# A graph attention layer's gather: visits of 64 target nodes instead of 125

## The chip, the cores and the metric

One core of one Trainium2 chip runs the whole program in one launch. The metric is device time in microseconds (us), here the median of three runs. A profiled execution of the same program gives the trace.

## The reference

The program is a graph attention layer with a residual, then a top-2 mixture of eight experts with a residual. The change concerns the first.

```python
xp = (x @ W).reshape(N, H, C)                 # N=3125 nodes, H=4 heads, C=256, 1024 columns in
a_src, a_dst = einsum(xp, att_src), einsum(xp, att_dst)          # N x H each
src, dst = edge_index[0] + loops, edge_index[1] + loops          # E=50000 edges, sorted by dst
e = leaky_relu(a_src[src] + a_dst[dst], 0.2)
m = segment_max(e, dst)
ee = exp(e - m[dst]); z = segment_sum(ee, dst)
out = segment_sum(xp[src] * (ee / z[dst])[:, :, None], dst)
x = x + relu(out + bias)                      # x was layer-normed before; then the experts
```

## The kernel before

The 3125 nodes are 25 **blocks** of 125, the 50,000 edges 391 **tiles** of 128. The edges are sorted by target, so a block's edges are consecutive; a tile that holds the border of two blocks is **visited** once for each, 391 + 25 = 416 visits in all. A visit takes 128 edges in the 128 partitions and adds what they bring to the sums of one block. Four visits are a group (104 groups).

**Projection** (0 to about 342 us, L303 to L714). For each tile of 125 nodes: layer norm on DVE (L458 to L487), transposes and products on PE (L664 to L683), high and low half-precision parts of the result (ACT L395, DVE L493), the terms of the nodes (DVE L508). POOL stores two arrays of 125 rows of 4096 bytes for each of the 25 tiles (L378, L380), and the stage of the layer's end one more. Between these, tile by tile and by hand (L624 to L654), DVE prepares the visits: 24 counts of edges below a block's border (`count`, L513, three in each of tiles 2 to 9), the visits' blocks and the words that tell where one begins and ends (`visits`, tile 11), the edges' numbers within their block (`edge_numbers`, tile 13; POOL fetches them with eight small gathers after tile 9, L370), three turns, eight parts of one-hots of the high part of the source (`high_one_hots`, L598, tiles 17 to 24), and the first chunk's tables (`build_first`, L609).

**Tables** (335 to 483 us, L760 to L875). In 8 chunks of 13 groups the node terms are selected for each edge: DVE turns numbers into one-hots in place (`build`, L776, L777: 128 x 6656 each), PE multiplies them with the terms (L865, L870), DVE picks and totals (L790, L800). SP loads the two arrays of each chunk (L767).

**Maxima and weights** (483 to 552 us, L895 to L1018). The result is PK: for each visit and edge the local target number (125 targets), the weights' high parts, a one, the weights' low parts.

**Gather** (552 to 1303 us, L1023 to L1145), the stage in question:
- POOL copies four columns of source numbers (L1047), waits for the row buffer's last use (`s_done`), and issues one indirect DMA a visit (L1052), 128 rows of 4096 bytes: the source's projected row, high part and low part. There are eight row buffers.
- DVE copies the group's packed weights (L1075, L1076), makes a one-hot of the target (L1083), and multiplies it with the four heads' high weights (L1087); ACT does the same with the low weights (L1113). Four buffers hold the one-hots, so DVE waits for `s_done` of the visit four before (L1082).
- PE adds into PSUM, for each head: high one-hot x high row, high x low, low x high, each 128 x 128 by 256 columns (L1130), then one product of 96 columns for the sums of the weights (L1135).
- At the end of a block DVE copies the sums to SBUF (`take`, L1066 twice 512 columns, L1067). It looks for ends after every second visit. PE waits before the first product of a new block until its half of PSUM is free:

```python
if first and h % 2 == 0 and not early(v, 1):
    pe.wait_ge(s_seen, 3 * v - 2 + h // 2)
for a, b in ((0, 0), (0, 1), (1, 0)):
    pe.matmul(main_ps[:, h * C:(h + 1) * C], O[:, k, 1 + HEADS * a + h, :],
              rows[:, 4 * p + k, b, h * C:(h + 1) * C], ...)
```

**Layer's end** (1303 to 1602 us), then **experts** (56 tiles of 128 slots, 7168 slots for 6250 pairs). The experts' three indirect DMAs a tile (L1403, L1726, L1732) carry `bounds_check=NODES - 1, oob_is_err=False`; empty slots have a number out of bounds. In that stage DVE splits the experts' weights with `scalar_tensor_tensor` on two SBUF operands (L1426) and also works with one operand in PSUM (L1757, L1767).

## Time and profile before

| what | value |
|---|---|
| median of 3 runs | 2163.4 us (2161.5 to 2164.1) |
| span of the profiled execution, first to last instruction | 2296.1 us |
| the profiled execution's own time | not given beside the span |
| busy in the span: PE, DVE, ACT, POOL | 1959.2, 1470.6, 1137.3, 768.2 us |
| mean granted clock of PE | 0.919 |
| DMA | 490.15 MB, mean 213 GB/s |

The rows are read so: a line number with L is a line of the kernel before; PE is TensorE, DVE VectorE, ACT ScalarE, POOL GpSimd, SP SyncE. A group's busy time is the union of its instructions, its mean that of one; the idle time is that of the engine just before them, with what ended it. "issue" is a wait for nothing that the profile shows. The granted clock is a share of 2.4 GHz.

### The profile page before, as it was taken

The page shows a single profiled execution, that of the slowest core. Times are in us where ns is not written, and L with a number is a line of the kernel's source. Part 1 is how long each engine was busy: PE and PEld are TensorE (multiplying, and loading weights), DVE is VectorE, ACT ScalarE, POOL GpSimd, SP SyncE. Part 2 cuts the span into 40 slices and gives each one's busy share as a digit, 9 for nine tenths or more (in the row PEclk, how much of TensorE's full clock was granted, in tenths as well). Part 3 has the DMA queues.
Part 4 walks back from the last instruction along what each step waited for, and adds up shares of the span by engine and source line. Part 5 has one row for each costly group of instructions (what it writes and reads, how often), then busy time and mean ns, then how long its engine had stood idle before and what let it go on. Part 6 is the DMA issues. An engine that isn't in the chain of part 4 may idle for free. (4 is left out here: it accounts for less than half of the span.)

```text
span 2296.1 us, 53233 instructions
## 1 busy us (share of the span) xinstructions
PE 1959.2 (85%) x14846; PEld 1318.7 (57%) x14847; DVE 1470.6 (64%) x4341; ACT 1137.3 (50%) x2499; POOL 768.2 (33%) x943
## 2 busy tenths in 40 slices
PE   6999977667878888888888589983899999999997
PEld 4666545645766667777667455652454445555553
DVE  7988859987666666666666699867543443443333
ACT  4444421113666666676666566654543443443332
POOL 1020000022555555555555232321233333333332
PEclk9999976568999999999999889995899999999999
DMA  7444544403988888888888677746646556644542
GB/s 272 134 143 136 172 131 172 186 0 114 312 281 291 286 299 287 294 296 287 287 298 294 235 249 240 228 142 234 233 169 249 212 167 239 221 160 171 176 162 80
DMA packets 135664, 490.15 MB, mean 213 GB/s; under 512 B 16900, under 2 KB 17108, under 8 KB 133410
## 3 DMA queue, kind: packets, MB, share of 16 engines
q0 software_dynamic: 95568, 334.62, 43.5%
q1 hardware_dynamic: 31954, 125.15, 15.1%
q10 hardware_dynamic: 8064, 29.36, 3.7%
q8 instruction: 47, 0.77, 0.1%
q14 instruction: 31, 0.25, 0.0%
HBM read 419.17 MB, written 81.17 MB: 218 GB/s over the span
## 5 line engine op out<-in xcount | busy, mean ns | idle before, releaser
L1130 PE MATMUL main_ps<-rows,O 128*128 128x256 f16 x4992 | 619.2, 283 | 125.7 <-DVE acc L1066 66.3
L1113 ACT ACTIVATE O<-O,pk 128x128 f16<-128x128 f16 x1664 | 502.9, 387 | 246.1 <-DVE O L1083 203.5
L1130 PEld LDWEIGHTS main_ps<-rows,O 128*128 128x128 f16 x4992 | 480.9, 102 | 217.9 <-issue 72.8
L1052 POOL DMA_INDIRECT rows<-projected,idx x416 | 395.5, 951 | 325.2 <-PE small_ps L1135 202.9
L1087 DVE TENSOR_SCALAR O<-O,pk 128x128 f16<-128x128 f16 x1664 | 314.6, 273 | 15.0 <-issue 0.2
L1837 PE MATMUL x_h<-w_p,gram 128*128 x1344 | 307.1, 386 | 18.4 <-ACT gram L1787 7.6
L1852 PE MATMUL x_o<-w_p,gram 128*128 x1344 | 308.0, 379 | 1.4 <-ACT gram L1806 1.4
L1886 PE MATMUL pj_ps<-gram,xsT 128*125 128x512 f16 x1200 | 271.1, 385 | 8.8 <-ACT xsT L402 5.5
L1837 PEld LDWEIGHTS x_h<-w_p,gram 128*128 128x128 f16 x1344 | 131.6, 99 | 171.6 <-issue 31.5
L1886 PEld LDWEIGHTS pj_ps<-gram,xsT 128*125 128x125 f16 x1200 | 163.2, 139 | 104.7 <-ACT xsT L402 8.6
L1083 DVE TENSOR_SCALAR O<-iota,pk 128x128 f16<-128x128 f16 x416 | 109.4, 263 | 164.9 <-PE small_ps L1135 124.1
L1852 PEld LDWEIGHTS x_o<-w_p,gram 128*128 128x128 f16 x1344 | 129.2, 98 | 147.1 <-issue 1.6
L1795 ACT ACTIVATE h_g<-h_b 128x512 f32<-128x512 f32 x56 | 35.3, 630 | 301.7 <-DVE h_b L1767 301.7
L1732 POOL DMA_INDIRECT out_dram<-x_y,xi x56 | 57.5, 1027 | 349.8 <-DVE x_y L1760 349.8
L1895 PE MATMUL n_pj<-gram,PK 128*128 128x512 f16 (+3 forms) x900 | 156.2, 330 | 13.3 <-ACT PK L1343 13.3
L1757 DVE SCALAR_TENSOR_TENSOR x_o<-x_o,b_t 128x1024 f32<-128x1024 f32 x56 | 69.0, 1233 | 135.4 <-PE x_o L1852 132.2
L1787 ACT ACTIVATE gram<-x_tr 128x2048 f16<-128x2048 f16 x56 | 105.1, 1878 | 58.3 <-PE x_tr L1904 55.0
L1895 PEld LDWEIGHTS n_pj<-gram,PK 128*128 128x128 f16 x900 | 83.8, 99 | 82.5 <-ACT PK L1343 15.9
L1760 DVE SCALAR_TENSOR_TENSOR x_y<-x_o,gate_of_slot,x_y 128x1024 f32<-128x1024 f32 x56 | 71.9, 1284 | 69.4 <-DMA x_y<-out_dram,xi 62.1
L1217 POOL TENSOR_TENSOR PK<-n_xn,PK 125x1024 f16<-125x1024 f32 x25 | 53.3, 2130 | 165.6 <-DVE n_x L1267 151.7
L1767 DVE SCALAR_TENSOR_TENSOR h_b<-x_h,b_b 128x512 f32<-128x512 f32 x56 | 38.7, 690 | 107.1 <-PE x_h L1837 104.3
L378 POOL DMA_DIRECT2D projected_f<-xp_f x25 | 13.2, 527 | 247.7 <-ACT xp_f L396 247.7
(346 smaller groups left out, 2538.9 us busy)
## 6 DMA issues: line engine op xcount, KB each, us to landing
w_f<-in_L_ffn_W_dram SPq DMA_DIRECT2D x14, 2048.0 KB
b_t<-in_L_ffn_b_dram ACTq DMA_DIRECT2D x56, 512.0 KB
projected_f<-xp_f POOLq DMA_DIRECT2D x25, 500.0 KB, 3.7
projected<-xp POOLq DMA_DIRECT2D x25, 500.0 KB, 4.6
out_dram<-n_x SPq DMA_DIRECT2D x25, 500.0 KB
x_after_gnn_normed<-PK POOLq DMA_DIRECT2D x25, 500.0 KB, 9.1
xt<-in_x_dram SPq DMA_DIRECT2D x24, 512.0 KB, 3.3
n_own<-projected_f SPq DMA_DIRECT2D x24, 512.0 KB, 13.0
```

Of the source, the lines that this page charges most:

```text
L1052: pool.indirect_dma_start(out=rows[:, 4 * p + k, :, :].rearrange("k n d -> k (n d)"), out_offset=None, in_=xp_d[:, :], in_offset=bass.Indi ...
L1083: dve.tensor_scalar(O[:, k, 0, :], iota16[:, :], pk[:, p, k, 0:1], None, ALU.is_equal).then_inc(s_oh, 1)
L1087: ins = dve.tensor_scalar(O[:, k, 1 + h, :], O[:, k, 0, :], pk[:, p, k, 1 + h:2 + h], None, ALU.mult)
L1113: ins = act.activation(O[:, k, 1 + HEADS + h, :], O[:, k, 0, :], ACT.Copy, scale=pk[:, p, k, w:w + 1])
L1130: pe.matmul(main_ps[:, h * C:(h + 1) * C], O[:, k, 1 + HEADS * a + h, :], rows[:, 4 * p + k, b, h * C:(h + 1) * C], start=first and h % 2 ...
L1757: dve.scalar_tensor_tensor(o_ps[:, p, :], o_ps[:, p, :], 1.0 / WS, b2_t[:, p, :], ALU.mult, ALU.add).then_inc(s_ob, 1)
L1760: dve.scalar_tensor_tensor(y[:, p, :], o_ps[:, p, :], at1(gateT, i), y[:, p, :], ALU.mult, ALU.add).then_inc(s_eo, 1)
L1787: act.activation(xgT[:, p, :, :, :], tr_ps[:, :, :, :], ACT.Copy).then_inc(s_xT, 1)
L1837: ins = pe.matmul(h_ps[:, :], xgT[:, p, a, k, :], w, start=(k == 0 and a == b), stop=(k == KD - 1 and a == 1))
L1852: ins = pe.matmul(o_ps[:, p, n * 512:(n + 1) * 512], hT[:, p, a, f, :], w, start=(f == 0 and a == b), stop=(f == KF - 1 and a == 1))
L1886: ins = pe.matmul(out, lhs[:, a, k, :], rhs[:, b, k, :], start=(k == 0 and a == b), stop=(k == last - 1 and a == 1))
L1895: ins = pe.matmul(out[:, cols], lhs[:, a, k, :], rhs[:, b, k, cols], start=(k == 0 and a == b), stop=True, skip_group_check=True)
```

## The change

A visit now serves one **sub-block**: nodes 0 to 63 or 64 to 124 of a block, 50 in all; 391 + 49 = 440 visits, 110 groups, 10 chunks of 11 groups. The stationary operand of a product holds a head's high and low one-hots side by side, 64 + 64 columns; two products a head (with the high and the low row) put the sums of both in the two halves of PSUM's partitions, one PSUM array for even and one for odd sub-blocks. One `scalar_tensor_tensor` on DVE makes all nine one-hots of a visit, in one of eight buffers; ACT has no part in the stage. At a block's end DVE moves one half across the partitions and adds the other, for both sub-blocks. Edges of a tile that lie outside the visit's sub-block get a source number past the last node, except in the first eight visits (visit = 4 x partition + q there, and `far` is zero in partitions 0 and 1), and the DMA's bounds check leaves them out. The counts are 49, five a tile in tiles 2 to 11, and what follows them moves by two tiles; the high one-hots come in five parts in tiles 20 to 24; the terms are copied once more, by sub-block.

```diff
-VISITS = TILES + BLOCKS
+SUB = 64
+SUBS = 2 * BLOCKS
+VISITS = TILES + SUBS - 1
...
-CHUNK = VISITS // 8
+CHUNKS = 10
+CHUNK = VISITS // CHUNKS
...
+SEEN = 9
...
-            PER = 3
+            PER = 5
...
-                        if i == 9:
+                        if i == 11:
                             rows_by_visit()
...
+                        dve.tensor_scalar(far[:, :], iota_col[:, :], 1.5, float(NODES), ALU.is_gt, ALU.mult)
+                        dve.tensor_scalar(out_f, fV[:, 3, :], -0.5, None, ALU.is_lt)
+                        link(dve.tensor_scalar(past_f, fV[:, 3, :], SUB - 0.5, None, ALU.is_gt))
+                        link(dve.tensor_tensor(out_f, out_f, past_f, ALU.add))
+                        dve.scalar_tensor_tensor(fV[:, 0, :], out_f, far[0:VP, :], fV[:, 0, :], ALU.mult, ALU.add).then_inc(s_vals, 1)
...
+                    def by_sub(n, bs):
+                        dve.wait_ge(s_st16, 2 * n + 2)
+                        dve.wait_ge(s_sub0, 1)
+                        of = st_sub[:, :, :].rearrange("k (b n) a -> k n b a", n=2)
+                        dve.tensor_copy(of[0:SUB, 0, bs, :], st16[0:SUB, bs, :])
+                        dve.tensor_copy(of[0:ROWS - SUB, 1, bs, :], st16[SUB:ROWS, bs, :])
...
-                        if 2 <= i < 10:
-                            for b in range(PER * (i - 2) + 1, PER * (i - 1) + 1):
+                        if 2 <= i < 12:
+                            for b in range(PER * (i - 2) + 1, min(PER * (i - 1) + 1, SUBS)):
                                 count(b)
...
-                        if i == 11:
+                        if i == 13:
                             visits()
-                        if i == 13:
+                        if i == 15:
                             edge_numbers()
-                        if i in (15, 17, 19):
-                            turned_numbers((i - 15) // 2)
+                        if i in (17, 18, 19):
+                            turned_numbers(i - 17)
...
-                        if 17 <= i < 25:
-                            high_one_hots(i - 17)
+                        if 20 <= i < 25:
+                            high_one_hots(i - 20)
...
-            O = sbuf(c, "O", [P, 4, 1 + 2 * HEADS, P], F16)
+            O = sbuf(c, "O", [P, 8, 1 + 2 * HEADS, SUB], F16)
...
-                                in_offset=bass.IndirectOffsetOnAxis(ap=idx[:, p, k:k + 1], axis=0)).then_inc(s_row[4 * p + k], 16)
+                                in_offset=bass.IndirectOffsetOnAxis(ap=idx[:, p, k:k + 1], axis=0),
+                                bounds_check=NODES - 1, oob_is_err=False).then_inc(s_row[4 * p + k], 16)
...
+                        for odd, own, off in ((0, low, up), (1, up, low)):
+                            for half in (slice(0, 512), slice(512, D)):
+                                dve.tensor_copy(other[own, half], main_ps[off, odd, half]).then_inc(s_seen, 1)
+                                n = n + 1
+                                wait_apart(dve, s_met, s_seen, n)
+                                dve.tensor_tensor(a(half)[own], main_ps[own, odd, half], other[own, half], ALU.add).then_inc(s_seen, 1)
+                                n = n + 1
+                            if odd == 0:
+                                for to, half_of in ((low, 0), (up, 1)):
+                                    ins = dve.tensor_copy(at(sacc, b)[to], small_ps[up, half_of, 0:2 * SUMS])
+                                ins.then_inc(s_seen, 1)
+                                n = n + 1
+                        wait_apart(dve, s_met, s_seen, n)
...
-                            if not early(i, 1):
-                                dve.wait_ge(s_done, v - 3)
-                            dve.tensor_scalar(O[:, k, 0, :], iota16[:, :], pk[:, p, k, 0:1], None,
-                                              ALU.is_equal).then_inc(s_oh, 1)
-                            dve.wait_ge(s_oh, v + 1)
-                            for h in range(HEADS):
-                                ins = dve.tensor_scalar(O[:, k, 1 + h, :], O[:, k, 0, :], pk[:, p, k, 1 + h:2 + h],
-                                                        None, ALU.mult)
-                            ins.then_inc(s_hi, 1)
+
+                            dve.scalar_tensor_tensor(
+                                O[:, 4 * p + k, :, :], iota16[:, 0:SUB].unsqueeze(1).broadcast_to([P, 1 + 2 * HEADS, SUB]), pk[:, p, k, 0:1],
+                                pk16[:, p, k, 1:2 + 2 * HEADS].unsqueeze(2).broadcast_to([P, 1 + 2 * HEADS, SUB]),
+                                ALU.is_equal, ALU.mult).then_inc(s_oh, 1)
...
-                @block.scalar
-                def _(act):
-                    def body(i, j, p):
-                        for k in range(4):
-                            act.wait_ge(s_oh, 4 * i + k + 1)
-                            for h in range(HEADS):
-                                w = 1 + SUMS + h
-                                ins = act.activation(O[:, k, 1 + HEADS + h, :], O[:, k, 0, :], ACT.Copy, scale=pk[:, p, k, w:w + 1])
-                            ins.then_inc(s_lo, 1)
...
-                                pe.wait_ge(s_seen, 3 * v - 2 + h // 2)
-                            for a, b in ((0, 0), (0, 1), (1, 0)):
...
+                                pe.wait_ge(s_seen, SEEN * (v - 1) + 2 + h)
+                            cols = slice(h * C, (h + 1) * C)
+                            for b in range(2):
+                                pe.matmul(of(main_ps, cols), O[:, 4 * p + k, 2 * h:2 * h + 2, :].rearrange("k n c -> k (n c)"),
+                                          rows[:, 4 * p + k, b, cols],
+                                          start=first and h % 2 == 0 and b == 0, stop=True, skip_group_check=True)
```

## Rows read from the trace of the kernel before

**Rows 1.** Stretches: us, busy of PE, PEld, DVE, ACT, POOL, clock, DMA share, GB/s.

```profile
74.10:85.00 10.90, 10.90 (x64) 7.07 (x63) 10.25 (x36) 5.15 (x9) 1.05 (x2) 1.00 0.50 145
129.90:140.40 10.50, 10.50 (x63) 7.05 (x62) 8.22 (x28) 5.14 (x8) 1.04 (x2) 1.00 0.50 147
...
335.40:482.70 147.30, 104.67 (x1428) 89.42 (x1424) 136.15 (x227) 23.79 (x105) 0.00 (x0) 0.58 0.40 157
552.50:1303.40 750.90, 624.06 (x5408) 522.78 (x5408) 474.16 (x2361) 502.85 (x1664) 416.08 (x519) 0.94 0.86 291
...
1615.00:2240.00 625.00, 611.75 (x3704) 312.59 (x3702) 262.56 (x234) 262.06 (x234) 207.50 (x255) 0.99 0.55 193
```

**Rows 2.** Groups, 552.5 to 1303.4 us: xcount, busy us, mean ns, idle us.

```profile
L1130 PE MATMUL main_ps<-rows,O 128*128 128x256 f16 x4992 | 619.2, 283 | 125.7 <-DVE acc L1066 66.3 <-issue 31.9 <-ACT O L1113 17.6
L1113 ACT ACTIVATE O<-O,pk 128x128 f16<-128x128 f16 x1664 | 502.9, 387 | 246.1 <-DVE O L1083 203.5 <-issue 41.9
...
L1052 POOL DMA_INDIRECT rows<-projected,idx x416 | 395.5, 951 | 325.2 <-PE small_ps L1135 202.9 <-issue 95.9 <-remote 22.6
L1087 DVE TENSOR_SCALAR O<-O,pk 128x128 f16<-128x128 f16 x1664 | 314.6, 273 | 15.0 <-issue 0.2
```

**Rows 3.** Timeline of PE, two visits in a row: start, length (us), engine, line.

```profile
904.69 0.21 PE L1135 MATMUL small_ps<-pk,O 128*128 128x96 f16 x1
...
906.04 0.21 PE L1135 MATMUL small_ps<-pk,O 128*128 128x96 f16 x1
```

**Rows 4.** Timeline around the end of a block, DVE and PE.

```profile
765.38 1.29 DVE L1066 COPY acc<-main_ps 125x512 f32 x2 [0.17 <-issue]
...
766.13 2.74 PE L1130 MATMUL main_ps<-rows,O 128*128 128x256 f16 x12 [3.23 <-ACT O L1113]
...
773.13 1.47 PE L1130 MATMUL main_ps<-rows,O 128*128 128x256 f16 x12
```

**Rows 5.** Timeline of POOL near the start of the gather.

```profile
558.23 0.96 POOL L1052 DMA_INDIRECT rows<-projected,idx  x1 [0.75 <-issue]
...
562.93 0.19 POOL L1047 COPY idx<-srcT 128x4 int32 x1
564.01 0.96 POOL L1052 DMA_INDIRECT rows<-projected,idx  x1 [0.90 <-PE small_ps L1135]
```

**Rows 6.** Groups of DVE, shapes apart, whole span.

```profile
L790 DVE TENSOR_TENSOR pick<-s_ps,PK 128x400 f32<-128x400 f32 x104 | 59.6, 574 | 10.5 <-PE d_ps L870 7.1
...
L1767 DVE SCALAR_TENSOR_TENSOR h_b<-x_h,b_b 128x512 f32<-128x512 f32 x56 | 38.7, 690 | 107.1 <-PE x_h L1837 104.3 <-issue 2.8
...
L513 DVE TENSOR_SCALAR_CACHE_REDUCE stage<-stage 98x512 f32<-98x512 f32 x24 | 16.4, 684 | 0.6
...
L777 DVE TENSOR_SCALAR one_hots<-one_hots,iota_col 128x6656 f16<-128x6656 f16 x4 | 7.8, 1946 | 0.0
...
L513 DVE DVE_READ_ACCUMULATOR stage<-stage 98x1 f32 x24 | 2.0, 83 | 0.0
```

**Rows 7.** Indirect DMAs on POOL by tile: ns min/median/max, first, last start.

```profile
L1403 POOL DMA_INDIRECT gram<-x_after_gnn_normed,xi x56: 1010/1012/2279, 1585.1 to 2251.6; - x56
...
L1726 POOL DMA_INDIRECT x_y<-out_dram,xi x56: 1014/1042/2207, 1602.3 to 2283.7; - x56
...
L1052 POOL DMA_INDIRECT rows<-projected,idx x416: 932/942/1028, 552.5 to 1292.5; - x139
```

**Rows 8.** Timeline of the expert stage, POOL beside DVE.

```profile
1635.13 4.48 DVE L1426 SCALAR_TENSOR_TENSOR w_p<-w_f,w_p 128x2048 f16<-128x2048 f32 x2
...
1636.13 1.33 POOL L1401 COPY xi<-token_of_slot 128x1 int32 x1
...
1638.29 2.23 POOL L1403 DMA_INDIRECT gram<-x_after_gnn_normed,xi  x1 [0.83 <-POOL xi L1401]
```

**Rows 9.** GB/s of the DMA engines in 40 slices of the span.

```profile
GB/s 272 134 143 136 172 131 172 186 0 114 312 281 291 286 299 287 294 296 287 287 298 294 235 249 240 228 142 234 233 169 249 212 167 239 221 160 171 176 162 80
```

**Rows 10.** The software DMA queue: packets, MB, share of 16 engines.

```profile
q0 software_dynamic: 95568, 334.62, 43.5%
```

226 lines of the change are left out of this document (126 added, 100 removed).

## The prediction

> **What bounds the kernel now.** I first cut the span into stages [rows 1]. From 552.5 to 1303.4 us the 416 visits of the gather run: 750.9 us, a third of the span, and the only long stretch that the change rewrites. In it PE is busy 624 us, the DMA engines 86%, POOL 416 us, so three resources are near each other. The groups of that stretch come next [rows 2]: 12 products a visit on PE (4992), four one-hots a visit on DVE and four on ACT, and one indirect DMA a visit on POOL, which is idle 325 us, 203 of them until PE frees a buffer. The timeline of PE says what a visit costs when nothing is late: 906.04 - 904.69 = 1.35 us [rows 3]; 416 of these are 562 us. At the end of a block PE stands until DVE has copied the sums out [rows 4]: the copy begins at 765.38, the next product at 766.13, after 3.2 us of idleness. So before, PE sets the pace and the 24 block ends add the rest (750.9 - 562 = 189 us).
>
> Right behind PE stands POOL. Where no buffer is missing, one group of four issues takes 564.01 - 558.23 = 5.78 us with its index copy [rows 5], 1.45 us a visit: only 0.10 us above PE's step. Whoever frees PE finds POOL next, and behind it DMA.
>
> **The change part by part.**
>
> 1. PE. Twelve products of 256 columns become eight, the small one stays: 12 x 256 + 96 = 3168 columns fall to 2144. Scaled from 1.35 us a visit takes 0.92 us; 440 visits 405 us. A block end holds PE longer: DVE copies 512 values, waits, adds 512 (0.69 us each, as the copy of 1.29 us for two in [rows 4] says), so about 1.8 us to the first product and some 4 us until the first visit is through. There is cover: eight row buffers at 1.6 us are 13 us, of which an issue, its landing and its product use about 6. PE is no longer the bound.
>
> 2. ACT loses all its one-hots (503 us busy [rows 2]); worth nothing by itself.
>
> 3. DVE. Five operations a visit become one scalar_tensor_tensor of 9 x 64 = 576 elements. A two-input operation of 400 elements takes 0.57 us, one of 512 takes 0.69 [rows 6]: 0.75 us for 576, about 0.68 from start to start. A group of four with its two copies is about 3.6 us, 110 groups 396 us. A block's taking grows from three operations to ten: four pairs of copy, wait and add at 1.4 us, two small copies and the last wait, some 6.2 us, 25 times 155 us. Together 551 us, under POOL's time. Behind a taking stand the next one-hots on DVE's queue; PE has two or three visits' worth made ahead, and then waits for at most 2 us, inside the cover of part 1.
>
> 4. POOL. 440 issues instead of 416, now with a bounds check. The check's price stands in another stage: the issue with bounds has a median of 1012 to 1042 ns, that without 942 [rows 7]. I take 0.07 us, 0.28 a group: 5.78 becomes 6.06 us. Then something that the gather stage does not show now. At 1638.29 POOL issues while DVE is in a scalar_tensor_tensor on two SBUF operands, and the issue takes 2.23 us, ending 0.9 us after that DVE operation; a one-column POOL copy beside the same kind takes 1.33 us [rows 8]; without it 1.01 is the rule [rows 7]. The new one-hot operation is of this kind, and runs 4 x 0.68 = 2.7 us of each group's 6.7, 40% of the time. An issue that falls into one waits on average half of it less 0.1, so 0.4 x 0.28 = 0.11 us; five POOL operations a group, with the copy at 0.15: 0.6 us. A group is 6.06 + 0.6 = 6.66 us, 110 groups 733 us, with 8 us for the last landing and product 741: **10 us less** than 750.9.
> Bounds: below, no hold and no check; then DMA holds it, 50,000 rows x 4096 bytes = 204.8 MB at the best slice's 312 GB/s [rows 9] = 656 us plus 8, 87 less. Above, every POOL operation meets a one-hot and waits 0.35 us: (6.06 + 5 x 0.35) x 110 + 8 = 867, 116 more. I take the middle value, since the held rows are of the same kind as the new operation and the length of the wait is the rest of the DVE operation.
> The Trainium skill (SBUF - State Buffer, "SBUF: two separate sides") says that a VectorE operation with two SBUF inputs keeps a GpSimd operation that reads SBUF off a shared port for its whole length. The rows agree, and by that rule this change brings a hold into the stage.
> The same section says that VectorE's fast modes on one input starve GpSimd's descriptor writing. By that rule the change would free POOL of a burden. The trace does not: beside 1664 fast one-hots of that sort the 416 issues last 932 to 1028 ns [rows 7]. I count no gain.
>
> 5. The rows not fetched. 391 tiles make 50,000 edges; 49 tiles are visited twice. A skipped row moves nothing: the software queue carried 334.62 MB [rows 10], whereas 416 x 128 rows, 75 stores of 125 rows and the 168 bounded transfers of the expert stage would be 344.6 MB at 4096 bytes each; there 3 x (7168 - 6250) = 2754 rows, 11.3 MB, lie out of bounds. So DMA gets 6% less than now, not more, and stays below POOL.
>
> 6. The projection stage. 49 counts instead of 24, five a tile in tiles 2 to 11. A count is 0.684 + 0.083 us, 0.73 from start to start [rows 6]. A tile with three counts lasts 10.9 us with DVE busy 10.25, one without 10.5 with 8.22 [rows 1], and PE full in both: DVE and PE tie. Two more counts add 1.45 us to each of eight tiles, 11.6; two tiles that had none become some 12.4 and 11.7, 3.1 more. The border arithmetic and the marking of outside edges (five passes over 512 values and some small links) stand on the same full DVE: 3 us. The queues of SP and POOL get the same transfers, two tiles later; POOL's eight small gathers stand behind the stores of tile 11 instead of 9, and nobody needs them before tile 15. Together **18 us**, 12 to 23.
>
> 7. The table stage. 147.3 us for 104 groups and seven builds [rows 1]; the builds are 7 x 3.9 = 27.3 [rows 6], a group 1.15. Six more groups are 6.9 us, nine builds of 5632 elements 29.7: +2.4. SP's loads are ten pairs instead of eight and shorter in the same measure as the time between two builds. With 1.5 for packing 440 visits instead of 416, **11 us**.
>
> 8. The last block is taken with nothing to cover it: 6.2 us against 1.5: **+4.5**.
>
> Sum: -10 + 18 + 11 + 4.5 = +23 us on the profiled span of 2296.1, so 2319. The runs' median is 2163.4, 133 us below that span; the page gives no time around it. In the expert stage PE is busy 612 of 625 us [rows 1], so the 133 us must lie elsewhere, some of them in the gather's idle PE. There the kernel before has more to shed than one paced by POOL. I add 8 us for that: 2163.4 + 23 + 8 = **2195**.
>
> **Rivals.**
>
> A, faster: POOL is not held. DVE runs its one-hots in bursts and then waits, and POOL may fall between them; the median bounded issue of the expert stage is 1012 ns, beside DVE operations of the same kind. Then a group is 6.06 us, the gather 667 + 8 = 675, -76; with 33.5 elsewhere -42: 2121. For it: the median. Against: the maxima of [rows 7] and the 133 us. If nothing else is paid, the floor of 664 gives 2110.
>
> B, much slower: PE's clock. Waiting 0.7 us in each visit and 4 us at a block end, PE may run at 1.2 GHz. In the table stage with short bursts of PE the granted clock was 0.58 [rows 1]; in the gather 0.94. At half clock a visit is 1.84 us, more than POOL's 1.67; 440 are 810 us, +59 and 33.5: 2256. It decides from the point where PE's visit exceeds POOL's step. Against: PE is then busy without a break, and in [rows 4] a visit's twelve products, 2.74 us after the stand, take 1.47 again seven microseconds later.
>
> C, no change: half the hold, gather -33, cancelled by the 33.5 elsewhere: 2163.
>
> D, the doubtful part does not do what it says: a skipped row takes a full row's time. 440 x 128 rows are 230.7 MB, at 312 GB/s 739 us: 2192, the forecast's own time by another path.
>
> **How the numbers follow.** Forecast 0.42 (own range 2168 to 2245), D 0.05, A 0.33 (2100 to 2150), B 0.10, C 0.10. A measurement of this kernel can tell 0.2%, 4 us, from no change. Slower: 0.42 + 0.05 + 0.10, less a little of the forecast's lower end, 0.56; faster A and a third of C, 0.36; within 0.2% 0.08. The range takes in A's middle and B's: 2110 to 2270.
>
> **What would show it.** Right: in the gather POOL's issues follow each other without a PE wait, at 6.4 to 6.9 us a group; many last over 1.1 us and end with a DVE one-hot; PE idles on rows; tiles 2 to 11 of the projection last 12.3 us. Wrong: issues at 1.01 us throughout and a gather under 690 us (A); a granted clock under 0.8 there (B); PE waiting for DVE's one-hots or its taking instead of rows (my cover is too thin); or a projection stage that does not grow.

## The result and the profile after

The kernel after takes 2430.9 us (median of 4 runs, 2428.6 to 2432.5), the kernel before 2162.6 (2161.5 to 2164.1): ratio 1.1248, interval 1.1232 to 1.1264, **268 us slower**. The forecast was 2195 us, its range ended at 2270. The sign was right, the size far off.

The profiled execution of the kernel after has a span of 2426.9 us, beside a run of 2428.6. The first profile of the kernel before, on which every price of the prediction rests, had 2296.1 us beside runs of 2163. So the kernel before was profiled again, unchanged.

> The kernel before, unchanged, profiled a second time. Its first profile had a span of 2296.1 us where its runs took 2163, and the prediction was priced from that profile. Theory P, the first profile was an execution that is not like the runs: the new span lies within 10 us of 2162, and the gather stage, with PE visits of 1.35 us, takes about 620 us instead of 750.9, since nothing else there has 130 us of idleness to lose. Rival, recording always lengthens this kernel: the span is near 2296 again and the gather near 750.

Its run took 2161.7 us, its span 2159.8. Theory P holds. The stretches of both, in the columns of [rows 1]; first the kernel before's second profile:

```profile
332.00:482.00 150.00, 107.03 (x1445) 91.56 (x1443) 136.87 (x229) 24.75 (x108) 2.25 (x1) 0.58 0.39 156
549.50:1173.00 623.50, 576.20 (x5408) 504.09 (x5408) 477.79 (x2359) 499.72 (x1664) 417.84 (x519) 0.99 0.96 350
1173.00:1475.00 302.00, 221.49 (x2060) 146.50 (x2060) 247.53 (x628) 175.42 (x263) 79.34 (x65) 0.86 0.66 223
```

and the kernel after:

```profile
343.00:508.00 165.00, 112.44 (x1560) 97.23 (x1560) 148.25 (x250) 25.48 (x113) 0.00 (x0) 0.57 0.43 158
585.00:1445.00 860.00, 554.06 (x3960) 388.83 (x3960) 509.56 (x908) 0.00 (x0) 520.53 (x549) 0.86 0.74 243
1742.00:2368.00 626.00, 609.13 (x3704) 312.13 (x3705) 262.25 (x233) 266.38 (x236) 207.22 (x254) 0.99 0.55 196
```

From here on "gather" is the time from the first row's issue to the start of the last small product: 622.8 us in the second profile of before (749.3 in the first), 853.8 after. The difference of the spans, 267.1 us, is **231.0 in the gather**, 35.5 ahead of it (the first row is issued at 585.0 instead of 549.5; 16.6 of them in the projection, 18.9 between there and the gather) and 0.6 behind it.

The groups of the gather after, beside [rows 2]:

```profile
L1185 PE MATMUL main_ps<-rows,O 128*128 128x256 f16 x3520 | 536.5, 304 | 302.1 <-issue 132.3 <-DVE O L1150 89.7 <-DVE acc L1128 69.9
L1106 POOL DMA_INDIRECT rows<-projected,idx x440 | 475.3, 1080 | 324.3 <-PE small_ps L1190 174.2 <-issue 96.7 <-POOL idx L1101 51.0
L1150 DVE SCALAR_TENSOR_TENSOR O<-iota,pk 128x576 f16<-128x576 f16 x440 | 332.3, 814 | 30.9 <-DVE pk L1144 22.0 <-PE small_ps L1190 3.5 <-DVE acc L1128 1.9
L1125 DVE COPY other_half<-main_ps 64x512 f32<-64x512 f32 x100 | 68.8, 688 | 125.7 <-PE small_ps L1190 123.4
```

and of the kernel before in its second profile:

```profile
L1130 PE MATMUL main_ps<-rows,O 128*128 128x256 f16 x4992 | 573.3, 273 | 48.8 <-DVE acc L1066 29.2 <-DMA rows<-projected,idx 9.3 <-issue 5.0
L1052 POOL DMA_INDIRECT rows<-projected,idx x416 | 397.3, 955 | 193.9 <-issue 79.8 <-PE small_ps L1135 68.0 <-POOL idx L1047 41.6
```

1472 products fewer, and PE is idle 302 us instead of 49. 132 of them wait for "issue", for nothing that the profile shows; 90 for one-hots; 70 for the taking of a block (`acc`), as the rows name them. POOL is the one that waits for PE (174 us), not PE for POOL. The mean product is 304 ns instead of 273, at a granted clock of 0.86 instead of 0.99.

**The "issue" waits.** The timeline of PE, far from a block end:

```profile
972.79 1.04 PE L1185 MATMUL main_ps<-rows,O 128*128 128x256 f16 x8 [0.42 <-DVE O L1150]
973.67 0.21 PE L1190 MATMUL small_ps<-pk,O 128*128 128x96 f16 x1
974.28 1.04 PE L1185 MATMUL main_ps<-rows,O 128*128 128x256 f16 x8 [0.40 <-DVE O L1150]
975.16 0.21 PE L1190 MATMUL small_ps<-pk,O 128*128 128x96 f16 x1
```

The products do stand as close as the prediction had them: 975.16 - 974.28 = 0.88 us for eight. But from one small product to the next it is 1.49 us, the array idle for some 0.6 of them. The row names a one-hot as what ended the wait, but none was late: DVE made four from 970.03 to 973.03, and the visits of 974.28 and after found them ready. It is so for most of the 89.7 us that the group's row puts down to one-hots: with each of the 132 visits set beside its own one-hot in the trace, 18 begin less than 0.5 us after it ended (33.6 us in all, behind block ends), the other 114 some 1.2 us or more after it (56.0 us). These 56 us belong to the "issue" waits. What PE's sequencer did in one such visit, by the view of the source lines from 974.9 to 976.4 us (count, duration in ns, start; the lines are the branch, a wait, the products and the small product):

```profile
L1201 PEldq COMPARE_BRANCH  x1: 207/207/207, 975.0 to 975.0; - x1
L1177 PEldq FUSED_REGOPS  x1: 42/42/42, 975.4 to 975.4; - x1
L1185 PEldq FUSED_REGOPS  x4: 46/46/46, 975.7 to 976.0; - x4
L1185 PEldq ALU_OP  x2: 36/36/36, 975.5 to 975.6; - x2
L1190 PEldq FUSED_REGOPS  x1: 46/46/46, 976.2 to 976.2; - x1
```

With three more ALU_OPs (two before the branch, one on L1176) they follow each other, some 0.1 us from start to start and 0.26 for the branch, and fill the whole 1.49 us. The six on L1185 and the one on L1190 are there because `odd`, the PSUM array of the visit, is a register: the address of each head's products is made anew. With fixed addresses (e3 below) these two lines have no such operation. The Trainium skill (Perfetto Trace Analysis, "Sequencer Loop") says that a sequencer passes an engine's instructions into a queue and executes control instructions itself; this trace adds what these cost.

**A block end.** DVE and PE:

```profile
961.31 0.69 DVE L1125 COPY other_half<-main_ps 64x512 f32<-64x512 f32 x1 [4.54 <-PE small_ps L1190]
963.34 1.03 PE L1185 MATMUL main_ps<-rows,O 128*128 128x256 f16 x4 [2.23 <-DVE acc L1128]
966.41 1.88 PE L1185 MATMUL main_ps<-rows,O 128*128 128x256 f16 x8 [0.53 <-issue]
967.58 0.69 DVE L1128 TENSOR_TENSOR acc<-main_ps,other_half 64x512 f32 x1 [0.21 <-DVE other_half L1125]
970.03 3.00 DVE L1150 SCALAR_TENSOR_TENSOR O<-iota,pk 128x576 f16<-128x576 f16 x4 [0.31 <-DVE pk L1144]
971.28 1.05 PE L1185 MATMUL main_ps<-rows,O 128*128 128x256 f16 x8 [1.63 <-DVE O L1150]
```

The block's last small product is at 960.89, the fourth of the next block at 972.16: 11.3 us for four visits. Four plain visits take 6.0 us. Three things follow each other: the stand until the first half is taken (2.23 us, and 0.40 for the second), two visits at half clock (four products in 1.03 us, eight in 1.88 us instead of 1.04; the granted clock from 962.2 to 969.0 is 0.50), and then, as the taking ends only at 968.3, a stand for one-hots. In the second profile of before such a place costs 1.7 us over two plain visits:

```profile
677.05 1.29 DVE L1066 COPY acc<-main_ps 125x512 f32 x2 [1.44 <-PE small_ps L1135]
677.80 1.48 PE L1130 MATMUL main_ps<-rows,O 128*128 128x256 f16 x12 [1.20 <-DVE acc L1066]
```

The first profile had a stand of 3.23 us at such a place and its next twelve products took 2.74 [rows 4].

### The profile page after: what moved, and what is told of

The parts are those of the page before. It is cut to its first block and busy times, and to the rows that moved or that the text cites. A ratio compares the mean times of both kernels' runs of the same rounds, so it can differ in the third digit from the quotient of the medians.

```text
span 2426.9 us, 50151 instructions
## 1 busy us (share of the span) xinstructions
PE 1890.0 (78%) x13470; PEld 1187.7 (49%) x13471; DVE 1543.0 (64%) x2967; ACT 635.7 (26%) x841; POOL 874.4 (36%) x981
## 3 DMA queue, kind: packets, MB, share of 16 engines
q0 software_dynamic: 99152, 324.99, 40.9%
## 5 line engine op out<-in xcount | busy, mean ns | idle before, releaser
L1185 PE MATMUL main_ps<-rows,O 128*128 128x256 f16 x3520 | 536.5, 304 | 302.1 <-issue 132.3
L1106 POOL DMA_INDIRECT rows<-projected,idx x440 | 475.3, 1080 | 324.3 <-PE small_ps L1190 174.2
L1185 PEld LDWEIGHTS main_ps<-rows,O 128*128 128x128 f16 x3520 | 341.1, 108 | 457.2 <-issue 387.9
L1150 DVE SCALAR_TENSOR_TENSOR O<-iota,pk 128x576 f16<-128x576 f16 x440 | 332.3, 814 | 30.9 <-DVE pk L1144 22.0
L1125 DVE COPY other_half<-main_ps 64x512 f32<-64x512 f32 x100 | 68.8, 688 | 125.7 <-PE small_ps L1190 123.4
L1143 DVE COPY pk<-PK 128x80 f16 (+1 forms) x110 | 23.7, 216 | 168.7 <-PE small_ps L1190 163.2
```

The lines of the kernel that those rows point to most:

```text
L1106: pool.indirect_dma_start(out=rows[:, 4 * p + k, :, :].rearrange("k n d -> k (n d)"), out_offset=None, in_=xp_d[:, :], in_offset=bass.Indi ...
L1125: dve.tensor_copy(other[own, half], main_ps[off, odd, half]).then_inc(s_seen, 1)
L1150: dve.scalar_tensor_tensor(O[:, 4 * p + k, :, :], iota16[:, 0:SUB].unsqueeze(1).broadcast_to([P, 1 + 2 * HEADS, SUB]), pk[:, p, k, 0:1], p ...
L1185: pe.matmul(of(main_ps, cols), O[:, 4 * p + k, 2 * h:2 * h + 2, :].rearrange("k n c -> k (n c)"), rows[:, 4 * p + k, b, cols], start=first ...
```

## The experiments

Ratios are against the kernel before. e1 is above. All others are changed kernels of one of two kinds: the kernel after with parts undone (e2 to e8, e10, e11, e17), and the kernel before with a suspected cost added or a wait taken away (e9, e12 to e16).

**e2_fixed_half.** Fixed addresses.

```diff
-                            odd = odd_at(k)
+                            odd = 0
```

> The kernel after, with every product of a visit put into the first PSUM half (a fixed address in place of one taken from a register); the second half is cleared once, so what belongs to odd groups of 64 nodes is added or overwritten in the first one: that part of the result is left out. Instructions of arrays, rows and taking stay. Theory S, PE's step of 1.49 us a visit is its sequencer's: one branch, one wait and seven register operations of about 0.1 us that build the PSUM addresses, with 0.6 us idle array. Without them the step is 0.9 to 1.0 us, the gather falls from 860 us to where POOL or DVE holds it, 680 to 740, the whole to 2250 to 2310 us. Rival, the 0.6 us come from the branch, or from waits for one-hots or rows: the step stays above 1.35 us and the whole within 30 us of 2431.

**e3_four_way.** Fixed addresses, nothing left out; the branch of the other visits is doubled in the same way. e5 to e8, e10, e11 and e17 contain this edit.

```diff
                             with pe.If(first_at(k) == 1):
-                                products(i, j, p, k, True, odd)
+                                with pe.If(odd == 1):
+                                    products(i, j, p, k, True, 1)
+                                with pe.Else():
+                                    products(i, j, p, k, True, 0)
...
```

> The kernel after, with fixed PSUM addresses got by a second branch on the half inside the branch on the first visit: the result is whole. Theory S: seven register operations (0.8 us) go, two and a branch (0.45 us) come, the step is 1.1 to 1.2 us, the gather 740 to 790 us, the whole 2310 to 2360 us. Rival, branches are what costs: the step is as long as now or longer, the whole 2431 or more.

**e4_short_taking.** The taking cut to three copies.

```diff
-                        for odd, own, off in ((0, low, up), (1, up, low)):
...
+                        for half in (slice(0, 512), slice(512, D)):
+                            dve.tensor_copy(a(half), main_ps[:, 0, half]).then_inc(s_seen, 2)
+                        dve.tensor_copy(at(sacc, b), small_ps[:, 0, 0:2 * SUMS]).then_inc(s_seen, 5)
```

> The kernel after, with the taking of a block cut to the kernel before's three copies out of the first half, 10 operations to 3; the adding of the halves and the second half's sums are left out. The register addresses on PE stay. Theory: the 24 block ends cost PE about 8 us each beyond its steps, and most of it is the taking and the one-hots queued behind it on DVE; cut by 5 to 6 us each, the gather falls by 120 to 145 us to 715 to 740, the whole to 2285 to 2310 us. Rival, the block ends are covered by PE's slow steps and POOL's: less than 50 us is gained.

Measured: e2 2334.6 us (ratio 1.0793, 1.0760 to 1.0826), gather 757.2; e3 2335.5 (1.0789, 1.0753 to 1.0824), gather 760.9; e4 2340.0 (1.0817, 1.0783 to 1.0852), gather 771.2. The register addresses are worth 93 to 97 us of the gather, the taking 83. The two causes are real and their rivals' bounds are passed, but only e3 came out as expected. The gathers of e2 and e4 are 17 and 31 us above the top of what their theories gave: what stands behind the removed cause holds earlier than was thought. In e2 a visit's steps are 0.92 us in the tenth percentile and 1.30 in the middle, and what ends PE's waits has changed:

```profile
L1187 PE MATMUL main_ps<-rows,O 128*128 128x256 f16 x3520 | 530.1, 310 | 218.9 <-DMA rows<-projected,idx 104.5 <-DVE acc L1128 68.8 <-DVE O L1152 34.7
```

The "issue" waits are gone, rows come late in their place: POOL's shortest group is 6.07 us, 1.52 a visit. That is the bound which the prediction had named, found behind the one it had missed. e4 tells of the clock too: some 660 of the 3519 steps from product to product last 0.21 us instead of 0.11 in the kernel after, 215 in e4, 18 in the kernel before (second profile). At 0.105 us each the half clock takes **70 us** after, 23 in e4, 2 before.

**e8_both_short** joins e3 and e4; **e11_three_causes** adds the edit of e7 to it.

> The four-way kernel with the short taking of e4_short_taking (three copies out of the first half; the halves are not added). The two causes found apart were worth 95 us (addresses) and 83 us (taking) of the gather's 854. Theory, they add until POOL holds the pace: gather 675 to 700 us, where POOL's 110 groups at 6.05 us and more (666 us) stand, whole 2250 to 2275 us. Rival, they overlap (both shorten the same stretches): gather above 730.

> e8_both_short with the compared row in PSUM: no register addresses, three-copy taking, no hold of POOL. In e8 POOL's groups are 6.61 us on average and PE waits 134 us for rows. Theory: POOL now paces, and each of its holds counts, so the hold, worth 12 us in e7 where PE paced half the time, is worth 25 to 50 us here: gather 680 to 705 us, near 110 x 6.07 = 668. Rival: the rows come late because of the DMA engines, not of POOL: less than 12 us gained.

e8: 2303.6 us (1.0674, 1.0641 to 1.0707), gather 731.2: the theory failed, its rival (above 730) came true by 1 us. Together the edits give 122.6 us, not the 176 of both alone. POOL's groups of 6.61 us on average are 727 us for 110: with PE's two causes gone this is the pace of a held POOL that part 4 of the prediction had put at 6.66 us and 741. e11: 2252.9 (1.0435, 1.0406 to 1.0463), gather 679.0, as its theory had it to 1 us: what e7 shows to be worth 12.6 us alone is worth 52.2 here. 110 groups of POOL at 6.08 us (its median in e11) are 669 us: this is POOL's pace.

**e7_iota_in_psum.** The hold of POOL, priced by [rows 8].

```diff
+                    dve.tensor_copy(iota_ps[:, 0:SUB], iota16[:, 0:SUB]).then_inc(s_iop, 1)
...
-                                O[:, 4 * p + k, :, :], iota16[:, 0:SUB].unsqueeze(1).broadcast_to([P, 1 + 2 * HEADS, SUB]), pk[:, p, k, 0:1],
+                                O[:, 4 * p + k, :, :], iota_ps[:, 0:SUB].unsqueeze(1).broadcast_to([P, 1 + 2 * HEADS, SUB]), pk[:, p, k, 0:1],
```

> The four-way kernel with the row of numbers that the one-hot operation compares with read from PSUM instead of SBUF, so that this DVE operation has one SBUF operand of a visit and one PSUM operand; the result is whole. Theory H, two SBUF operands hold POOL: its issues fall from a mean of 1097 ns to about 1010, its index copies from 330 ns to about 200, 50 us of POOL's time in all, and the gather falls by 20 to 50 us unless the DVE operation becomes much longer. Rival, the long issues come from something else (descriptor writing against the rows' traffic): mean and copies stay.

2323.1 us (1.0761, 1.0733 to 1.0788), gather 748.3. POOL's issues by tile (min/median/max) in e3 and in e7:

```profile
L1106 POOL DMA_INDIRECT rows<-projected,idx x440: 984/1009/1620, 585.3 to 1339.3; - x147
```

```profile
L1108 POOL DMA_INDIRECT rows<-projected,idx x440: 984/991/1092, 586.4 to 1327.0; - x147
L1103 POOL COPY idx<-srcT x110: 187/193/207, 585.3 to 1321.9; 128x4 int32 x108, 128x4 int32<-128x4 int32 x2
```

The mean issue falls from 1097 to 995 ns and the mean index copy from 330 to 195: 4 x 0.102 + 0.135 = 0.54 us a group, where the prediction had taken 0.6. Theory H is right in cause and in POOL's times, but the gather goes down by only 12.6 us, less than the 20 to 50 expected, since PE paced. The Trainium skill (SBUF - State Buffer, "SBUF: two separate sides") has this hold for a VectorE operation with two SBUF inputs; the trace agrees, and with one of the two in PSUM there is none.

**e6_all_rows.** No bounds check, outside rows fetched.

```diff
-                                in_offset=bass.IndirectOffsetOnAxis(ap=idx[:, p, k:k + 1], axis=0),
-                                bounds_check=NODES - 1, oob_is_err=False).then_inc(s_row[4 * p + k], 16)
+                                in_offset=bass.IndirectOffsetOnAxis(ap=idx[:, p, k:k + 1], axis=0)).then_inc(s_row[4 * p + k], 16)
...
-                        dve.tensor_scalar(far[:, :], iota_col[:, :], 1.5, float(NODES), ALU.is_gt, ALU.mult)
+                        dve.tensor_scalar(far[:, :], iota_col[:, :], 1.5, 0.0, ALU.is_gt, ALU.mult)
```

> The four-way kernel with no bounds check on the gathers and with the outside edges' rows fetched (no one-hot matches them, so the result is whole). Theory: the check costs POOL 0.06 us an issue, its shortest group falls from 6.05 to 5.8 us; 12% more rows are moved, 230.7 MB, which at the 345 to 360 GB/s of the kernel before's second profile take 640 to 670 us, under the gather's 761. The gather falls by 10 to 25 us. Rival, DMA is near: rows land later, PE waits for rows, and the gather stays or grows.

2331.8 us (1.0785, 1.0748 to 1.0823), gather 756.4 against 760.9: neither theory's gain nor the rival's loss; the medians of the runs differ by 3.7 us, less than the runs of either kernel among themselves. The check costs 1009 - 957 = 52 ns an issue by the medians, POOL's shortest group falls from 6.05 to 5.76 us (0.28 was forecast). The software queue carried 347.23 MB instead of 324.99, so the skipped rows do move nothing. PE waits for rows as long as before (35.6 us, 35.7 in e3). The edit changes two things at once; that neither is worth time here is the simplest reading, a gain from the check that hides a loss from the rows is not ruled out.

**e5_taken_later.** The ends of blocks looked at two visits later (the index steps shift with it).

```diff
-                                        wait_apart(dve, s_met, s_done, v + u - k - 1)
+                                        wait_apart(dve, s_met, s_done, v + u - k - 3)
-                                            take(block_at(u), v + u - k - 2)
+                                            take(block_at(u), v + u - k - 4)
```

> The four-way kernel (e3_four_way, gather 761 us) with a block's taking put two visits later in DVE's order, behind the one-hots of the fourth or fifth visit after the block's last instead of the second or third; the eight one-hot buffers allow it, and the result is whole. Theory: after a block end PE runs out of one-hots while DVE is in the taking (39 us of PE idle on one-hots in e3); two more visits made ahead cover 2 x 0.92 us of each of 24 block ends, so the gather falls by 25 to 50 us to 710 to 735, the whole from 2335 to 2285 to 2310. Rival: POOL's issuing, at 6.5 us a group, is what paces e3, and less than 12 us is gained.

2319.4 us (1.0735, 1.0703 to 1.0766), gather 741.5: 19.4 us, short of the 25 to 50, above the rival's 12. PE's waits that are named for one-hots fall from 39.2 to 13.9 us, and waits for rows (76.8 us) take their place.

**e10_after_all** joins e3, e5, e7 and moves POOL's index copies to ACT:

```diff
-                        pool.tensor_copy(idx[:, p, :], srcT[:, sl]).then_inc(s_idx, 1)
+                        act.copy(idx[:, q, :], srcT[:, sl]).then_inc(s_idx, 1)
...
```

> The kernel after with every repair that leaves the result whole: fixed addresses by four ways, taking two visits later, the compared row in PSUM, and index copies on ACT (idle there). Theory: the causes found apart add as far as the next engine allows: POOL's group 5.2 to 5.6 us, PE 440 visits of 0.92 to 1.2 us and block ends of some 5 us; gather 640 to 690 us, whole 2215 to 2265 us, still above the kernel before's 2160, since the stages ahead cost 35 us more. Rival: the block ends alone hold it, gather above 710 us.

2292.0 us (1.0620, 1.0584 to 1.0656), gather 713.5: above the 640 to 690 of the theory, as its rival had it in time, but not by its cause alone. POOL's median group is 5.19 us, 571 us for 110, so POOL no longer holds the stage as a whole. The four visits from each of the 24 block ends take 254 us in all, 2.65 us each; the others still take 1.32 us on average where the array needs 0.92, and "issue" waits of 81.5 us are left beside 72.0 for the taking. With two branches a visit PE's sequencer comes round in 1.16 us where nothing is late (e3, branches at 904.45, 905.62, 906.77), and takes longer at the first visit of a group. So the block ends and the sequencer hold it together, with POOL's 1.30 us a visit right behind. One end:

```profile
1128.77 0.61 PE L1213 MATMUL main_ps<-rows,O 128*128 128x256 f16 x4 [2.39 <-DVE acc L1138]
1130.39 1.01 PE L1213 MATMUL main_ps<-rows,O 128*128 128x256 f16 x4 [1.01 <-DVE acc L1138]
1132.12 1.89 PE L1213 MATMUL main_ps<-rows,O 128*128 128x256 f16 x8 [0.65 <-issue]
1133.89 1.04 PE L1213 MATMUL main_ps<-rows,O 128*128 128x256 f16 x8
```

After two stands in a row the products run at 1.2 GHz: four in 1.01 us, then eight in 1.89, against 1.04. It is so behind each of the 24 ends (some 510 slow steps, nearly all within 12 us of a taking's start).

**e9_before_act_index.** The same move of the index copies, in the kernel before.

> The kernel before, with the index copy of each group moved from POOL to ACT two groups ahead (four index buffers, the waits on landed rows go with it; the result is whole). In the kernel before's second profile POOL's group, 5.84 us median, is longer than four visits of PE, 5.41 us, and the gather of 623 us is 104 such groups. Theory: POOL is what bounds the kernel before; its group falls to 4.9 to 5.4 us, PE becomes the bound, gather 585 to 605 us, whole 2125 to 2145 us. Rival: the copy was hidden, or ACT brings it late: whole within 6 us of 2160 or longer.

2159.5 us, ratio 0.9998 (0.9985 to 1.0011), gather 622.7. POOL's median group fell from 5.84 to 5.41 us, exactly four visits of PE, and nothing else moved: my theory was wrong, its rival right. PE bounded the kernel before.

**e12_before_49_counts.**

```diff
-            PER = 3
+            PER = 5
+            COUNTS = 49
...
```

> The kernel before with the projection stage's counting as the kernel after has it: 49 counts instead of 24, five a tile, and the index steps that follow them two tiles later (25 counts' results are not used; the result is whole). The prediction priced counts at 14.7 of its 18 us for this stage; between the two kernels the stage grew by 16.6 us. Theory: DVE has no room in these tiles, the stage and the whole grow by 10 to 17 us, to 2170 to 2177. Rival: the counts are mostly covered and the 16.6 us are the border arithmetic: less than 5 us.

2174.8 us (1.0075, 1.0051 to 1.0099); the first row is issued at 565.7 instead of 549.5, 16.2 us later, and the gather is the same 622.8. The counts, with the steps two tiles later, are 16.2 of the 16.6 us by which the projection grew; border arithmetic and marking show next to nothing.

**e13_before_register.** The converse of e2: register addresses put into the kernel before (`of` is the kernel after's, and takes array `odd` of two by `bass.ds`).

```diff
-                                pe.matmul(main_ps[:, h * C:(h + 1) * C], O[:, k, 1 + HEADS * a + h, :],
+                                pe.matmul(of(main_ps, slice(h * C, (h + 1) * C)), O[:, k, 1 + HEADS * a + h, :],
...
```

> The kernel before with the PSUM address of each product built from a register, as the kernel after does it (the register is always 0, the work and the result are the same). Theory S, a visit on PE takes the longer of its products (1.35 us for 13) and its sequencer's instructions: 0.7 us of branch, waits and word, 2 + 5 register operations of 0.1 to 0.12 us, and what it takes to pass on 26 array instructions. In the kernel after the sum was 1.49 us with 18 of these, so here 1.5 to 1.7 us: the gather grows from 623 to 640 to 700 us, whole 2180 to 2240. Rival, there is enough cover under 13 products: steps stay 1.35, whole within 6 us of 2160.

2326.6 us (1.0754, 1.0729 to 1.0779), gather 787.4: **165 us for one register in an address**, beyond even what theory S gave.

```profile
904.75 1.48 PE L1134 MATMUL main_ps<-rows,O 128*128 128x256 f16 x12 [0.93 <-DVE O L1090]
906.06 0.21 PE L1139 MATMUL small_ps<-pk,O 128*128 128x96 f16 x1
906.36 1.48 PE L1134 MATMUL main_ps<-rows,O 128*128 128x256 f16 x12
907.68 0.21 PE L1139 MATMUL small_ps<-pk,O 128*128 128x96 f16 x1
```

The step is 1.62 us instead of 1.35, as forecast; the gather is above its 640 to 700. The sequencer's branch comes round in the same time (905.50, 907.14). 416 x 0.27 are 112 us. The other 50 come with the first visit of a group, where the loop's branch and the load of the visit word come on top (2.33 us on average, 1.53 in the kernel before): a quarter of all steps are 2.08 us or more, against 1.35 in the kernel before.

**e14_before_two_halves, e15_halves_act_index, e16_group_branches.** The kernel before with two PSUM halves for even and odd blocks, so that PE does not wait for the block before. In e14 a second branch a visit picks the half; e15 moves the index copies too; e16 tests once a group:

```diff
+                        with pe.If(odd_at.some > 0):
+                            apart()
+                        with pe.Else():
+                            with pe.If(odd_at(0) == 1):
+                                for k in range(4):
+                                    products(i, j, p, k, False, 1)
...
```

> The kernel before with two PSUM halves, even blocks in one and odd blocks in the other, chosen on PE by a second branch with fixed addresses; PE's first visit of a block no longer waits for the taking of the block before, only for visits five back. The result is whole. Theory: the 24 stands (30 us idle on the taking, and 20 to 30 us of what follows them) go, and the second branch hides under 13 products: PE 416 x 1.35 = 563 us; but POOL's 104 groups of 5.84 us are then the bound, 607 plus 8: gather 610 to 618 us, whole 5 to 12 us less than before. Rival A: stands were covered by nothing else, gather 570 to 600. Rival B: the second branch makes the visit longer than 1.35 us, no gain or a loss.

> e14 with the index copies on ACT as in e9, so neither the taking nor POOL holds PE. Theory: the two edits are worth nothing or little apart and something together: POOL's group is 5.0 us where it may be, PE's four visits 5.41, gather 570 to 590 us, whole 2110 to 2130 us, faster than both kernels by 30 us or more. Rival: another resource (DVE, ACT's copies, rows from DMA at 360 GB/s) holds near 1.45 us a visit: gather above 605 us.

> e15 with one test a group in front: where no visit of a group of four is the first of its block (80 of 104 groups), one branch on the half leads to four visits in a row without branches; the others go as in e15. The result is whole. Theory S: the sequencer then runs ahead under 13 products a visit, the four visits take 5.41 us, the stands stay away, gather 580 to 605 us, whole 2115 to 2145 us, below both kernels. Rival: DVE and ACT, which make 9 one-hots a visit in about 1.4 us, are met at 1.45 us a visit: gather 605 to 625, whole as before.

e14 2191.5 us (1.0139, 1.0118 to 1.0160), gather 650.2; e15 2193.5 (1.0157, 1.0126 to 1.0188), 653.0; e16 2179.0 (1.0083, 1.0062 to 1.0104), 639.8. All three miss: e14 is rival B's loss, e15 its rival's, e16 is above both theory and rival. No wait for the taking is left, yet the gather is longer than 622.8 in each. In e14 the median step is 1.41 us, and

```profile
L1135 PE MATMUL main_ps<-rows,O 128*128 128x256 f16 x4978 | 587.2, 274 | 58.7 <-ACT O L1117 33.7 <-DVE O L1091 10.3 <-issue 7.5
```

By this row PE now waits for one-hots (33.7 and 10.3 us), for which it hardly waited before. As in the kernel after, the name is right only for a part. With each wait set beside its one-hots, 19 of them (17.0 us) end with a late one-hot, against 4 (2.1 us) in the second profile of before; the other 50 (27.0 us) do not, and 47 of these stand before the first visit of a group. One of them, with what the sequencer did just before it, by source line from 906.9 to 908.9 us (L92 is the loop, L133 the visit word, L1148 and L1154 the two branches):

```profile
L92 PEldq COMPARE_BRANCH  x1: 208/208/208, 907.1 to 907.1; - x1
L133 PEldq TENSOR_LOAD <-visit_words x1: 311/311/311, 907.5 to 907.5; - x1
L1148 PEldq COMPARE_BRANCH  x1: 207/207/207, 908.1 to 908.1; - x1
L1154 PEldq COMPARE_BRANCH  x1: 75/75/75, 908.5 to 908.5; - x1
```

```profile
908.89 1.48 PE L1135 MATMUL main_ps<-rows,O 128*128 128x256 f16 x12 [0.64 <-DVE O L1091]
```

Its last one-hot had ended at 906.7. So the second branch hides under 13 products in three visits of four (1.42 us on average, 1.47 in the kernel before) and not behind the loop and the word: the first visit of a group takes 1.95 us on average instead of 1.53, 44 us for 104 groups, more than the 27 by which the gather grows (most of the 17 us of late one-hots are in these 44). With a branch once a group (e16) the median step is 1.35 again, but the first visit of a group is still 1.91; of the waits named for one-hots 18.4 us are real there. That the stands of the kernel before were also time in which DVE and ACT got ahead fits the 17 and 18 us; no run shows it alone. No edit here beats the kernel before.

**e17_after_groups.** The test a group, in e10.

> e10_after_all (the kernel after with every repair, gather 713 us) with the same test a group: 60 of its 110 groups hold no first visit of 64 nodes and run without branches. Theory S: there a visit falls from 1.2 to 1.3 us to 0.92, a group by 1.2 to 1.6 us in all, 60 groups 70 to 95 us; POOL's groups of 5.19 us (571 us in all) and the 24 block ends of some 5 us each stop it earlier: gather 650 to 690 us, whole 2230 to 2265. Rival: block ends and their half clock hold it, PE only waits elsewhere: gather above 700.

2271.1 us (1.0501, 1.0479 to 1.0522), gather 694.3. The gain is 19 us, where the theory had 23 to 63: 4 us above its range and below the rival's 700. This is the fastest kernel of the new design that leaves nothing out, some 110 us slower than the kernel before and 160 faster than the change as made.

## Why the prediction was wrong

The forecast missed by 236 us. By its own steps:

- **The base** (the sum and the 8 us behind it): 120 us. The 10 us less for the gather were counted from 750.9 us. The 133 us between profile and runs were seen, and the text even said that some of them lie "in the gather's idle PE", but gave them 8 us. The second profile has 126.5 of them in the gather (749.3 - 622.8). A gather of 741 us, as forecast, is 118 more than 622.8, and would by itself have made the forecast some 2315. The evidence was in the rows: 416 x 1.35 = 562 us of PE and 104 x 5.78 = 601 of POOL, with nothing else in the stage that a run 133 us shorter could have given up.
- **Part 1, PE:** 113 us, with part 3 (the gather's 854 - 741). "A visit takes 0.92 us" was scaled by columns. The columns were right (0.88 us for eight products), the visit is 1.49. "PE is no longer the bound" fell with it. Without the register addresses the gather is 761 us (e3), without the long taking as well 731 (e8). The registers on PE were in the diff; they were not priced, because in [rows 3] the same sequencer's branch and waits were invisible, hidden under 13 products.
- **Part 3, the taking:** 6.2 us were forecast, 7.0 measured (961.31 to 968.3). The stands themselves were sized about right: 18 waits for one-hots of 1.9 us on average (33.6 us), and 2.9 us an end for the taking (69.9). What failed is "inside the cover": PE had no slack to cover them, since its own step of 1.49 us is within 0.03 us of POOL's shortest (6.05 us a group), and the half clock behind each stand was not in the sum. e4 puts the taking at 83 us, half clock included.
- **Rival B** was refused with the argument that PE would be busy without a break. The rival is wrong as a state of the whole stage and right piecewise: a burst at half clock behind each block end, 70 us in all. The Trainium skill (TensorE: Matmul & The Clock Gate, "HAM oscillation - how this bites in real kernels") describes a kernel whose every wait brings back the lower clock; the trace agrees, with 0.50 granted behind the stand at 961 us and 0.86 in the whole gather.
- **Part 4, POOL:** cause and size right (hold 0.54 us a group for 0.6, check 0.29 for 0.28). It was the second bound and not the first: only where PE's two causes are gone does POOL set the pace, with the hold at 731 us (e8, forecast 741) and without it at 679 (e11, rival A's 675). Rival A fell in the kernel after, whose issues average 1080 ns.
- **Part 5:** right in that the skipped rows move nothing, and e6 shows no gain in time from them. The 312 GB/s that the lower bound and rival D took as a ceiling was none: the kernel before's second profile moved 350 GB/s over its gather.
- **Part 6:** right in size, 16.6 us for 18, but 16.2 of it is the counts (e12), which had 14.7. **Part 7** was mis-sized: 18.9 us for 11. By the two profiles the table stage grew by 12.1 us and the stage of maxima and weights by 6.8, for which the sum had 1.5; no run takes these apart. **Part 8:** 0.6 for 4.5, in a stretch that differs by 10 us among executions of kernels that don't change it, so neither is shown.
- **Rival C** was added up wrongly: with half the hold the gather is 6.36 x 110 + 8 = 708 us, 43 less and not 33. With the 8 us of the forecast its 2163 stands.

The base's 120 (118, and the 2 by which 8 falls short of 10), the gather's 854 - 741 = 113, and 3 in parts 6 to 8 make the 236.

Its list of what would show it wrong did name the case: "PE waiting for DVE's one-hots or its taking instead of rows (my cover is too thin)"; its price was missing. The sign came out right, but not by the gather: it was forecast 10 us shorter and is 231 us longer. What was right for the reason given are the 33.5 us elsewhere, measured 36.1.

What stays open is why the first profile of the kernel before was 136 us longer. Its stands at block ends are twice as long, and there are passages where products come two at a time with no work or semaphore late,

```profile
757.63 0.38 PE L1130 MATMUL main_ps<-rows,O 128*128 128x256 f16 x2 [0.28 <-issue]
758.37 0.49 PE L1130 MATMUL main_ps<-rows,O 128*128 128x256 f16 x3 [0.37 <-issue]
```

in the middle of a visit. The second profile has next to none (5.0 us of "issue" against 31.9), and nothing here says what held them. Open, too, is how the 231 us part among causes that overlap: by single removals 93 to 97 (addresses), 83 (taking), 13 (hold, from e3); by the last step of a chain the hold alone is 52.

## What to carry to other kernels

Before fewer products are counted as less time, list what the engine's sequencer does in a visit (branches, waits, register operations, at some 0.1 us each and 0.26 for a branch) and take the longer of this sum and the products' time. Here the sequencer was hidden under 13 products with fixed addresses (1.35 us) and was the bound at 9 (1.49 us), and a register in a PSUM address is paid for each head. Where a row names a late operand, look up when that operand ended: of the 90 us named for one-hots 56 were the sequencer's. Where a profile is longer than the runs beside it, find the idle time that the runs don't have before anything is subtracted from it. PE, standing at each block's end, paid three times: the stand, the half clock behind it, and whatever was queued behind the taking.

## Not expected of the hardware

A register operation on PE's sequencer is recorded with 36 to 46 ns but takes its place for about 100; a compare and branch 207 ns recorded, 265 in place (in some places 75 and 133). The same address from a register cost 93 us of the gather over 440 visits of 9 products (e3, net of a second branch) and 165 us over 416 visits of 13 (e13). A DVE operation with one operand moved to PSUM kept its length (811 ns, 814 before) and freed POOL of its hold: no issue above 1092 ns, of 440, where the longest had been 1620.
